# Routing of a last mixture-of-experts stage in two halves of tokens, with both weightings of the choice on the vector engine

## The reference, cut to what matters

```python
def _L3_ffn_ref(x, router_w, router_b, expert_w, expert_b):
    B, N, D, C, E, K = (8, 2048, 32, 32, 8, 2)
    router_probs = jax.nn.softmax(x @ router_w + router_b, axis=-1)
    top_p, top_i = jax.lax.top_k(router_probs, K)
    top_p = top_p / jnp.sum(top_p, axis=-1, keepdims=True)
    expert_out = jnp.einsum('bnd,edc->bnec', x, expert_w) + expert_b
    gathered = jnp.take_along_axis(expert_out, top_i[..., None], axis=2)
    return jnp.einsum('bnk,bnkc->bnc', top_p, gathered)
...
    x = x + _L3_conv_ref(_ln_c(x), ...)
    t = _to_tokens(x)
    t = t + _L3_ffn_ref(_ln_t(t), L3_ffn_router_w, L3_ffn_router_b, L3_ffn_expert_w, L3_ffn_expert_b)
    x = _from_tokens(t, x)
```

## Time and profile before

| | us |
|---|---|
| three runs | 593.43, 594.74, 594.96 |
| median | 594.74 |
| the profiled execution, device time | 593.35 |
| its span, first to last instruction | 591.6 |
| TensorE busy (loading of weights) | 453.9 (351.1) |
| VectorE busy | 383.3 |
| GpSimd busy | 247.9 |
| ScalarE busy | 238.0 |
| mean granted clock of TensorE | 0.864 of full speed |

### The profile page before, as it was taken

How to read it: one execution, slowest core, us unless ns; L and a number is a source line. 1 busy time by engine, 2 the same in 40 slices (tenths; PEclk the granted TensorE clock), 3 DMA queues, 4 the chain that set the end, 5 groups by cost and what they waited for, 6 DMA issues and landing times.

```text
span 591.6 us, 8640 instructions
## 1 busy us (share of the span) xinstructions
PE 453.9 (77%) x3018; PEld 351.1 (59%) x3018; DVE 383.3 (65%) x1231; ACT 238.0 (40%) x573; POOL 247.9 (42%) x309
## 2 busy tenths in 40 slices
PE   3688867998598856698569995889769866908996
PEld 2356743686344743498449984479646755905664
DVE  5796497725897498401963449910679489398885
ACT  1576544401476535375450003557459652200000
POOL 2696287000566087100150001400148478218995
PEclk9999978687788988899958998979869995567999
DMA  9200000000000000000000000000000000000323
GB/s 169 60 2 1 1 1 0 1 2 0 1 1 1 1 1 2 0 2 1 2 0 1 2 1 1 1 1 1 2 1 1 2 1 1 0 0 7 49 37 53
DMA packets 34106, 6.03 MB, mean 10 GB/s; under 512 B 33644, under 2 KB 33772, under 8 KB 34029
## 3 DMA queue, kind: packets, MB, share of 16 engines
q1 hardware_dynamic: 34062, 5.46, 5.3%
HBM read 3.36 MB, written 2.10 MB: 9 GB/s over the span
## 4 chain that ended last, share of the span: by engine, by line
PE 50%; DVE 36%; ACT 5%; POOL 4%; issue 3%; DMA 1%; SPq 1%; DVEq 0%; POOLq 0%
DVE moments L290 7%; PE psum L1242 7%; DVE ab L659 5%; PE psum L1004 5%; DVE z L298 5%; PE psum L1003 5%; PE psum L542 4%; PE psum L392 4%; DVE ab L645 4%; PE psum L1415 3%; PE psum L553 3%; POOL z L330 2%; PE psum L1393 2%; PE psum L512 2%; PE psum L1435 2%
## 5 line engine op out<-in xcount | busy, mean ns | idle before, releaser
L330 POOL TENSOR_TENSOR z<-z,stats 128x496 f32<-128x496 f32 (+1 forms) x64 | 67.9, 1062 | 128.6 <-DVE z L298 128.6
L392 PE MATMUL psum<-ident,z 128*128 128x128 f32 x256 | 57.0, 366 | 46.5 <-POOL z L330 45.2
L392 PEld LDWEIGHTS psum<-ident,z 128*128 128x128 f32 x256 | 39.9, 189 | 76.8 <-POOL z L330 64.2
L512 PE MATMUL psum<-wp_L,z_t 64*128 64x320 f32 x384 | 67.2, 478 | 5.7 <-DVE ab L659 2.8
L290 DVE BATCH_NORM_STATS2 moments<-x_cols 128x6 f32<-128x64 f32 x448 | 61.9, 210 | 2.0 <-POOL x_cols L715 1.7
L319 ACT ACTIVATE z_t<-psum 128x512 f32<-128x512 f32 x56 | 40.1, 720 | 43.9 <-PE psum L392 43.8
L327 POOL MEMSET z<- 128x16 f32 x32 | 4.0, 125 | 122.6 <-DVE z L298 122.6
L512 PEld LDWEIGHTS psum<-wp_L,z_t 64*128 64x128 f32 x384 | 36.1, 197 | 31.8 <-issue 26.6
L1095 ACT ACTIVATE ab<-psum,mv 128x128 f32<-128x128 f32 x112 | 41.1, 367 | 20.1 <-PE psum L1004 9.8
L1004 PE MATMUL psum<-ab,R_vt 128*128 128x128 f32 x224 | 48.9, 302 | 0.0
L298 DVE TENSOR_TENSOR z<-x_cols,moments 128x496 f32<-128x496 f32 (+1 forms) x56 | 47.9, 855 | 0.0
(11 more groups left out here) (241 smaller groups left out, 920.4 us busy)
## 6 DMA issues: line engine op xcount, KB each, us to landing
x_cols<-in_x_dram SPq DMA_DIRECT2D x16, 128.0 KB, 3.0
out_dram<-x_cols SPq DMA_DIRECT2D x32, 64.0 KB, 1.9
par<-in_par_dram SPq DMA_DIRECT2D x1, 644.5 KB
w<-in_w_dram SPq DMA_DIRECT2D x1, 264.0 KB
w<-in_w_dram SPq DMA_DIRECT2D x1, 256.0 KB
mask<-in_mask_dram SPq DMA_DIRECT2D x1, 64.0 KB
row<-in_row_dram SPq DMA_DIRECT2D x1, 3.3 KB
w2l<-in_w2l_dram SPq DMA_DIRECT2D x1, 2.0 KB
```

Of the source, the lines that this page charges most:

```text
L330: pool.tensor_tensor(Z4[:, r, :, 0:c], Z4[:, r, :, 0:c], RSTD[:, q].unsqueeze(3).to_broadcast([N, SQ, G, c]), ALU.mult).then_inc(L.s["z"], 1)
L392: m = pe.transpose(bank(b % 2)[:, k * N:(k + 1) * N], block_of(Z)(4 * b + k), ident[:, :])
L512: m = pe.matmul(bank(slot_bank(s) + h, 2 * 5 * C), ZT[rows, s, :], wp[l][rows, :, :], start=True, stop=True)
```

## The change

The routing on VectorE is done for tokens 0 to 63 of each partition (blocks 0 to 15, whose logits are bank 6) and then for tokens 64 to 127 (bank 7), each with the whole sequence of instructions at half the width. TensorE signals twice, behind `route(3)` and behind `route(7)`, and the two halves on VectorE wait for one signal each. ScalarE makes the two weights for each half. GpSimd's multiplication of the first choice by its weight is gone; VectorE does it. The count of `top` for which `add_up(0)` waits goes from 6 to 20, which is the last reading of the logits in the new order: 14 counted instructions of the first half and 6 of the second.

```diff
@@ f3_pe
                 if b >= 3:
-                    route(b - 1)
+                    m = route(b - 1)
+                    if b == S // 8:
+                        m.then_inc(L.s["rt_ps"], 1)
             wait_all(pe, L.banks_free)
             route(7).then_inc(L.s["rt_ps"], 1)
@@ f3_act
-            act.wait_ge(L.s["diff"], L.at["diff"] + 1)
-            act.activation(W1S, DIF, ACT.Sigmoid).then_inc(L.s["sg"], 1)
-            act.activation(W2S, DIF, ACT.Sigmoid, scale=-1.0).then_inc(L.s["sg"], 1)
+            for h in range(2):
+                n = slice(h * N // 2, (h + 1) * N // 2)
+                act.wait_ge(L.s["diff"], L.at["diff"] + h + 1)
+                act.activation(W1S[:, n], DIF[:, n], ACT.Sigmoid).then_inc(L.s["sg"], 1)
+                act.activation(W2S[:, n], DIF[:, n], ACT.Sigmoid, scale=-1.0).then_inc(L.s["sg"], 1)
@@ f3_dve
-            dve.wait_ge(L.s["rt_ps"], L.at["rt_ps"] + 1)
...
-            choose(LOGITS, M1, R1M, RT[1], RANK1)
-            then(dve.scalar_tensor_tensor(out=RT[2], in0=RT[1], scalar=-FAR, in1=LOGITS, op0=ALU.mult, op1=ALU.add))
-            choose(RT[2], M2, R2M, RT[3], RANK2, second=True)
-            dve.wait_ge(L.s["sg"], L.at["sg"] + 2)
-            then(dve.tensor_tensor(RT[3], RT[3], per_e(W2S), ALU.mult))
-            dve.wait_ge(L.s["hot"], L.at["hot"] + 1)
-            then(dve.tensor_tensor(RT[4], RT[5], RT[3], ALU.add))
+            for h in range(2):
+                tokens = slice(h * N // 2, (h + 1) * N // 2)
+                m1, m2, dif, w1s, w2s = (t[:, tokens] for t in (M1, M2, DIF, W1S, W2S))
+                first, rest, second, both = (RT[k][:, tokens, :] for k in (1, 2, 3, 4))
+                dve.wait_ge(L.s["rt_ps"], L.at["rt_ps"] + h + 1)
+                choose(LOGITS[:, tokens, :], m1, R1M[:, tokens], first, RANK1[:, tokens, :])
+                then(dve.scalar_tensor_tensor(out=rest, in0=first, scalar=-FAR, in1=LOGITS[:, tokens, :], op0=ALU.mult,
+                                              op1=ALU.add))
+                choose(rest, m2, R2M[:, tokens], second, RANK2[:, tokens, :], (dif, m1))
+                dve.wait_ge(L.s["sg"], L.at["sg"] + 2 * h + 2)
+                then(dve.tensor_tensor(first, first, per_e(w1s), ALU.mult))
+                then(dve.tensor_tensor(second, second, per_e(w2s), ALU.mult))
+                then(dve.tensor_tensor(both, first, second, ALU.add))
@@ f3_pool
-            pool.wait_ge(L.s["sg"], L.at["sg"] + 1)
-            pool.tensor_tensor(RT[5], RT[1], W1S.unsqueeze(2).to_broadcast([N, N, E3]), ALU.mult).then_inc(L.s["hot"], 1)
```

More of the change, by code:

```diff
@@ L229, in build @@
         t3 = stage("L3", "norm weights ones tri", src=XC, scratch=XR, eps=0, e2=EPS)
-        f3 = stage("F3", "norm ones turn", "w_dve w_pe rank hot rt_ps top diff sg e_ps e_mul e_half e_last e_quart e_sum done", src=XC, eps=1, e2=0.0)
+        f3 = stage("F3", "norm ones turn", "w_dve w_pe rank rt_ps top diff sg e_ps e_mul e_half e_last e_quart e_sum done", src=XC, eps=1, e2=0.0)
         x_done = lambda L: [(L.s["done"], L.at["done"] + S // 4)]
@@ L1354, in build @@
         HALVES = Z[:, :].rearrange("p (j e k f) -> p j e k f", j=4, e=E3 // 2, k=2)
-        F3_LOGITS_READ = 6
+        F3_LOGITS_READ = 20
         LOGITS = bank(6, n=2).rearrange("p (n e) -> p n e", e=E3)
@@ L1466, in per_e, with choose @@
             def per_e(t):
-                return t.unsqueeze(2).to_broadcast([N, N, E3])
-            ranks = rank[:, :].unsqueeze(1).to_broadcast([N, N, E3])
+                return t.unsqueeze(2).to_broadcast([N, N // 2, E3])
+            ranks = rank[:, :].unsqueeze(1).to_broadcast([N, N // 2, E3])
             dve.wait_ge(L.s["rank"], L.at["rank"] + E3)
-            dve.wait_ge(L.s["rt_ps"], L.at["rt_ps"] + 1)
-            def choose(logits, m, rm, hot, r, second=False):
+            def choose(logits, m, rm, hot, r, dif=None):
                 then(dve.tensor_reduce(m, logits, AX.X, ALU.max))
-                if second:
-                    dve.tensor_tensor(DIF, M1, M2, ALU.subtract).then_inc(L.s["diff"], 1)
+                if dif is not None:
+                    dve.tensor_tensor(dif[0], dif[1], m, ALU.subtract).then_inc(L.s["diff"], 1)
                 then(dve.tensor_tensor(r, logits, per_e(m), ALU.is_equal))
```

## The result

The changed kernel takes 586.73 us in the median of four runs (585.69 to 589.26), the kernel before 594.09 us (592.95 to 594.96): a ratio of 0.989 with a 95% interval of 0.9858 to 0.9922. Forecast were 588.0 us and a range of 586.0 to 590.2.

The account below looks back on a forecast made before the run. A serial 17.12 us VectorE routing chain, waiting for the last logits, was taken as the bound. Starting its first half early saves 6.7 us: 593.35 - 6.7 = 586.65, with the median 1.39 above, 588.0 us; range 586.0 to 590.2.

Parts of the forecast that it names:

- The chain and the idle time: Routing: 17.12 us of serial VectorE instructions after the last logits, with VectorE idle 8.92 us before; first half starts about 507.0.
- The price of a half: VectorE's routing of one half: 12 steps at 0.72, two bf16 products at 0.45, one difference at 0.14; 9.68 us.
- The estimate of about 8.5 us: A half's length on VectorE by the skill page's cycle table, saving 8.6 us; the prediction stayed with the trace rows.
- The removed product: GpSimd's weighting moved to VectorE: 1.64 us back on the second bf16 product, 1.25 added, worth 0.4 us.
- The price of halving: Fixed part of VectorE's routing steps paid twice: 19.36 us against 16.73 unhalved, 2.6 us more work.
- The sum: First weigh at 526.4 instead of 533.1, 6.7 us earlier; 586.65 us profiled, 588.0 us predicted median.
- The covers: Time to spare before VectorE needs ScalarE's weights: 0.7 us in the first half, 1.5 in the second.
- The last scaling on GpSimd: Layer norm's end, beside the first half's first two steps, which read PSUM: no cost, 0.3 us as upper bound.
- TensorE's clock: Experts' start after an 8.6 us idle time: clock lost and regained as before, no gain or loss expected.
- The same slow restart: TensorE's first expert products after the idle time run at the low clock for 4.85 us, as before.
- The bound of 0.8 us either way: Change of the end if the experts' slow stretch is 1.65 us shorter or longer.
- a slow stretch shorter or longer changes the end by about half: Experts' start: low-clock products take 1.9 times as long, so 1.65 us of slow stretch moves the end 0.8 us.

Follow-up runs that it names:

- the kernel without the overlap: The changed kernel with both halves waiting for the last logits, so nothing runs beside the turns; 597.12 us, ratio 1.0046 to the kernel before.
- the interleaved kernel: The changed kernel with the first half's weighings started early and one second-half step behind each; 583.7 us, ratio 0.9797 to the kernel before.
- the first of the two kernels that keep TensorE busy: The changed kernel with the first two blocks' expert products made five times instead of once; 587.55 us, ratio 0.9887 to the kernel before.
- one step ahead: The interleaved kernel with the second half's first step put ahead of the first weigh; 584.28 us, ratio 0.9866 to the kernel before.
- two steps: The interleaved kernel with two second-half steps behind each weighing of blocks 0 to 7; 587.93 us, ratio 0.9896 to the kernel before.

## Why the prediction was right, point by point

- **The chain and the idle time.** VectorE's 8.92 us of idle time were usable to the whole, and the first half starts 0.08 us before the centring's end. Right, and shown by the kernel without the overlap: 9.00 us.
- **The price of a half**, forecast 9.68, measured 9.74 us: steps of 0.69 us and 0.73 from start to start (taken: 0.72), bf16 products of 0.42, difference 0.14. The estimate of about 8.5 us is out: at 512 elements a waiting step is 0.69 us from SBUF and from PSUM alike. It came from a table on the page "VectorE: DVE Perf Modes" of the Trainium skill. Below that table, in the same section, the page says that its VectorE row comes out too short, and gives 691 ns for an fp32 `tensor_tensor` of 512 elements. The prediction used the table alone; the 691 ns agree with the rows.
- **The removed product**, forecast 0.4 us net: 0.39.
- **The price of halving**, forecast 2.6: 2.74.
- **The sum**, 6.7 us earlier at the first `weigh`: 26.05 - 19.40 = 6.65, or from the parts -0.39 + 2.74 - 9.00 = -6.65. The medians differ by 7.4, the spans of the two profiles by 4.1, since the stages ahead took 2.5 us more in the profile after. Against the profiled execution (589.26 us) the sum of 586.65 is 2.6 us short, for the same reason. The forecast of 588.0 for a median of 586.73 is off by less than the runs of one kernel differ; that the median came so near is in part luck, the 6.65 us are not.
- **The covers.** ScalarE's weights had 1.0 us to spare in the first half (forecast 0.7). The last scaling on GpSimd (509.69 to 510.71) lay beside the two steps that read PSUM and cost nothing.
- **TensorE's clock.** The same slow restart: right. The bound of 0.8 us either way was too wide on the side of the gain: the slow stretch gone altogether puts TensorE 1.2 us ahead and brings 0.36 us. The error is in the step "a slow stretch shorter or longer changes the end by about half": it reckoned with TensorE alone, while GpSimd's sums start with the first `weigh` whatever the clock, and its last one holds up VectorE's last sum.
- **The missed thing.** That the experts of the first 16 blocks could start with the first half's weights stood in the same rows and was not seen. It brings 4.5 us more, where the change brought 6.6.

## What to carry to other kernels

An idle engine in front of a serial chain is worth the chain's length that fits in, minus the fixed part of each extra instruction. Both come from rows of the trace, the second from the same operation at two widths (here 0.15 us, and 0.03 for each wait), and each was right within 0.15 us. Splitting without overlap is a loss, so look whether the first part's inputs are complete when the engine falls idle, and then also whether the first part's consumers can start. Compare two profiles from the last point at which they do the same thing, not by their spans: that point moved by up to 6.7 us between the profiles here (503.08 to 509.78), though the code ahead of it is the same, and the choice behind it by 0.02 us in two profiles of one kernel.

## What the runs showed of the hardware

- A step of VectorE with both inputs in SBUF and one of GpSimd do not share. Where GpSimd's began first, VectorE's ended a fixed time after it: 0.54 or 0.55 us for a step of 0.68 or 0.69 alone (the second bf16 product before, 1.28 and 1.77 above), 0.28 for one of 0.42 or 0.43 (1.18 and the 1.37 of the last quarter sum). Where VectorE's began first (533.51, 0.68 us, in the interleaved kernel), GpSimd's took 1.79 us instead of 1.27. The Trainium skill, page "SBUF — State Buffer", section "Who interferes with whom", describes this as a lock held for the whole instruction; the rows agree.
- TensorE's granted clock can fall within a stretch of work. In the first of the two kernels that keep TensorE busy it was 0.60 in 531 to 535 us, where TensorE was busy for 3.84 of 4 us, after idle times of 1.84 and 0.42 us ahead. It also fell behind an idle time of 1.95 us (one step ahead) and behind 1.25, 1.05 and 1.76 us (two steps). With 0.98, 0.42 and 0.61 us, and through idle times of up to 1.12 us in the interleaved kernel, it stayed at 1.00. Whether the length of a gap or its place in time decides was not told apart.
- Where the 1.5 to 7 us between runs of one kernel come from stays open. In the profiles they lie ahead of the changed stage: behind the last centring the two profiles of the changed kernel agree within 0.05 us.
